# Latent attention of one core: the row probabilities are normalised on GpSimd in place of VectorE

## What is computed

```python
xn = _layernorm(x, axis=-1)
q = (x @ wq).reshape(Bq, Tq, N_KV, N_REP, HEAD_DIM)          # x is xn here; 2 key heads, 4 query heads each
k = einsum('bkhl,ld->bkhd', k_lat, wk_up); v = einsum('bkhl,ld->bkhd', v_lat, wv_up)
scores = einsum('bqhrd,bkhd->bhrqk', q, k) * scale           # Tq = 1024, causal
probs = softmax(where(causal, scores, min), axis=-1)
y = einsum('bhrqk,bkhd->bqhrd', probs, v)
return y.reshape(Bq, Tq, N_HEADS * HEAD_DIM) @ wo
x = x + attention(xn) + six_layers(xn)
```

## Time and profile before

| | |
|---|---|
| median of 3 runs | 1861.76 us |
| span of the profiled execution | 1864.6 us |
| TensorE matmul busy | 1689.0 us (91%) |
| VectorE busy | 1577.2 us (85%) |
| ScalarE busy | 1373.5 us (74%) |
| GpSimd busy | 1395.7 us (75%) |
| latent attention, first to last masked row | 36 to 341 us |

### The profile page before, as it was taken

One profiled execution on the slowest core, in us unless ns is written; L12 is line 12 of the kernel. 1 busy time (PEld: TensorE's weight loads), 2 busy tenths in 40 slices (PEclk: granted clock), 3 DMA queues, 4 the chain that ended last, 5 costly groups with the idle time before them and its releaser, 6 DMA issues.

```text
span 1864.6 us, 74251 instructions
## 1 busy us (share of the span) xinstructions
PE 1689.0 (91%) x31196; PEld 1143.3 (61%) x31196; DVE 1577.2 (85%) x2292; ACT 1373.5 (74%) x2048; POOL 1395.7 (75%) x1493
## 2 busy tenths in 40 slices
PE   6878787788899999999999999999999999999995
PEld 4656666455566666666666566656666666666664
DVE  5867668689898999998999889999899898999973
ACT  3667668466777887788777787788778877887773
POOL 3323223598799888998889888889888889888871
PEclk9999999899999999999999999999999999999997
DMA  4000000001000010000100001000001000000000
GB/s 139 2 0 0 0 1 1 1 28 32 7 7 15 8 56 7 11 15 7 55 7 12 14 7 55 7 7 12 14 30 32 7 12 14 7 8 7 7 7 27
DMA packets 41652, 31.97 MB, mean 17 GB/s; under 512 B 31040, under 2 KB 38912, under 8 KB 39680
## 3 DMA queue, kind: packets, MB, share of 16 engines
q1 hardware_dynamic: 41344, 27.48, 5.0%
HBM read 20.13 MB, written 1.05 MB: 11 GB/s over the span
## 4 chain that ended last, share of the span: by engine, by line
PE 37%; DVE 19%; issue 11%; POOL 7%; ACT 6%; DVEq 0%; POOLq 0%; ACTq 0%
PE banks L1147 15%; PE banks L1401 9%; PE banks L1350 4%; PE banks L1425 4%; PE banks L1386 4%; DVE arena L1012 3%; DVE lnx L1074 3%; DVE small L1041 3%; DVE small L1047 2%; DVE small L1035 2%; DVE small L1059 2%; DVE arena L1007 1%; POOL arena L544 1%; ACT L820 1%; ACT arena L754 1%
## 5 line engine op out<-in xcount | busy, mean ns | idle before, releaser
L1401 PE MATMUL banks<-M,xs 128*32 128x512 f32 x3072 | 369.2, 598 | 0.6 <-ACT arena L754 0.3
L1007 DVE TENSOR_TENSOR arena<-banks,tabs 128x1024 f32<-128x1024 f32 x192 | 233.8, 1218 | 34.1 <-ACT arena L714 17.8
L490 POOL TENSOR_TENSOR arena<-arena 128x1024 f32<-128x1024 f32 x96 | 229.8, 2394 | 43.7 <-DVE arena L1012 43.5
L754 ACT ACTIVATE arena<-banks 128x1024 f32<-128x1024 f32 x192 | 196.9, 1025 | 67.9 <-PE banks L1401 66.8
L1012 DVE TENSOR_TENSOR arena<-banks,tabs 128x1024 f32<-128x1024 f32 x192 | 233.2, 1215 | 0.0
L495 POOL TENSOR_TENSOR arena<-arena 128x1024 f32<-128x1024 f32 x96 | 228.1, 2376 | 0.0
L485 POOL TENSOR_TENSOR prob<-prob,small 128x1024 f32<-128x1024 f32 x96 | 183.8, 1915 | 29.9 <-DVE small L1049 29.9
L1074 DVE SCALAR_TENSOR_TENSOR lnx<-lns,small 128x128 f32<-128x128 f32 x96 | 175.2, 1825 | 34.8 <-POOL small L538 33.7
L1147 PE MATMUL banks<-qkH,xsH 128*128 128x512 f32 x384 | 173.6, 452 | 29.9 <-DVE arena L1012 28.1
L1425 PE MATMUL banks<-arena 128*32 128x128 f32 x6144 | 191.0, 277 | 5.4 <-ACT arena L820 4.2
L410 POOL TENSOR_TENSOR gqs<-arena,cst 128x128 fp32r<-128x128 f32 x112 | 45.1, 403 | 200.9 <-PE banks L1147 171.1
(11 more groups left out here) (123 smaller groups left out, 4033.1 us busy)
## 6 DMA issues: line engine op xcount, KB each, us to landing
arena<-in_wvo_dram SPq DMA_DIRECT2D x6, 1024.0 KB, 5.2
qkraw<-in_wqk_dram SPq DMA_DIRECT2D x6, 1024.0 KB, 5.2
lns<-Xt SPq DMA_DIRECT2D x96, 32.0 KB
lns<-Xt SPq DMA_DIRECT2D x96, 31.8 KB
W<-in_w_dram SPq DMA_DIRECT2D x6, 341.0 KB, 3.4
lns<-Xt SPq DMA_DIRECT2D x84, 0.2 KB
W<-in_w_dram SPq DMA_DIRECT2D x6, 192.0 KB, 3.4
res<-in_x_dram SPq DMA_DIRECT2D x4, 256.0 KB, 3.8
```

What stands on the lines that cost most here:

```text
L490: pool.tensor_tensor(kc, kc, ks, ALU.add).then_inc(s["k_add"], 1)
L754: act.activation(vw[:, (2 * k + g) % RV, :], two(V_BANK), ACT.Copy).then_inc(s[f"v_cp{g}"], 1)
L1007: dve.tensor_tensor(heads(c), heads(two(0)), table(k % NT, kind), ALU.mult).then_inc(s[done], 1)
L1401: ins = pe.matmul(bk(V_BANK + z)[WIN * q:WIN * (q + 1), :], xs[:, b, t0:t0 + WIN], M[:, q, :, :].rearrange("p m n -> p (m n)"), start=True ...
```

## The change

`normalise` leaves VectorE and becomes a GpSimd `tensor_tensor` with the reciprocal broadcast along the row, in the same place in memory. GpSimd's body becomes: the query split of row ahead(j), then the normalisation of row j. The splits of rows 0 and 2 stand ahead of the loop. Nothing else moves; all waits on ls_rec and ls_nrm keep their counts.

```diff
             def latent(it, tables):
-                for k, j in enumerate(apart):
+                def part(j):
+                    k = apart.index(j)
                     i, h = bodies[j]
...
+                def normalise(j):
+                    pr = probs_of(j)[:, 0:(bodies[j][0] + 1) * P]
+                    pool.wait_ge(s["ls_rec"], CR + it * len(bodies) + j + 1)
+                    pool.tensor_tensor(pr, pr, gst[:, 16 + bi(j):17 + bi(j)].to_broadcast([P, pr.shape[-1]]), ALU.mult).then_inc(s["ls_nrm"], 1)
+
+                for j in (0, 2):
+                    part(j)
+                for j in range(len(bodies)):
+                    if ahead(j) in apart:
+                        part(ahead(j))
+                    normalise(j)
...
-                def normalise(j):
-                    pr = probs_of(j)[:, 0:(bodies[j][0] + 1) * P]
-                    dve.wait_ge(s["ls_rec"], CR + it * len(bodies) + j + 1)
-                    dve.tensor_scalar(pr, pr, gst[:, 16 + bi(j):17 + bi(j)], None, ALU.mult).then_inc(s["ls_nrm"], 1)
...
                 for j in range(len(bodies)):
-                    normalise(j)
                     if ahead(j) is not None:
                         cap(ahead(j))
```

More of the change, by code:

```diff
@@ L207, in build @@
             "act": "x_init kk_cp m_cp va_cp wvo_cp gm_cp lq_cp lvl_cp ls_exp lt_cp ly_cp".split(),
-            "dve": "lo_add st_bn st_ag st_eps ln_x0 rs_0 ls_cap ls_max ls_neg ls_rec ls_nrm".split(),
-            "pool": "zeroed gx_H gx_L gq_H gq_L".split(),
+            "dve": "lo_add st_bn st_ag st_eps ln_x0 rs_0 ls_cap ls_max ls_neg ls_rec".split(),
+            "pool": "zeroed gx_H gx_L gq_H gq_L ls_nrm".split(),
         }
```

## The result

The changed kernel takes 1876.45 us (median of 7 runs, 1873.59 to 1879.42), the kernel before 1861.76 us (7 runs, 1856.19 to 1870.29). The ratio is 1.0075, 95% interval 1.0054 to 1.0097: slower, by some 14 us. The profiled execution took 1876.55 us with a span of 1874.7, 10.1 us above the span before.

The account below looks back on a forecast made before the run. A loop of waits, the short normalisation behind the long row's maximum, was taken to bound the kernel. 2.5 us in each of three iterations (7.5) plus 3.7 in the fourth gave +11.2 us, 1873 us; range 1865 to 1881.

Parts of the forecast that it names:

- The price: Normalisation on GpSimd: 0.18 us + 0.00169 us a column, 2.31 us a pair; with two splits 4.05 us a pair.
- The loop of rows (7,0): Long row's finish, scores, mask, reciprocal, GpSimd normalisation: 3.7 us a pair, so +0.3 us for m = 0 to 3.
- m = 4 to 7: Between finishes of long rows 4 and 7: 4.35 us, then two GpSimd-bound pairs of 4.05, sum 12.45 against 12.09, +0.4.
- 11 to 13: Between finishes of long rows 11 and 13: output matmuls on TensorE set the pace before and after, difference 0.
- 13 to 14: Between finishes of long rows 13 and 14: 3.8 us against 4.29, -0.5, the only place where position outweighs GpSimd's slowness.
- The tail: Iteration's end: finish(S_14) 1.9 us later instead of 1.44, +0.45; the last two normalisations hidden behind the next iteration's queries.
- The fourth iteration: Last latent-attention iteration: +3.7 us, including +1.1 at the start and +1.2 for line 424 before L_7's normalisation.
- The signs: Changed profile: GpSimd busy +148 us to about 1543, VectorE about 1508, iteration about 82 us, little GpSimd idle in rows (6,1) to (4,3).
- Absorbed: Rival, chance 0.12: iteration starts and ends take up the lag; only the fourth's 3.7 us or less remain, 1864 to 1865.
- Faster: Rival, chance 0.06: GpSimd's normalisation runs ahead, half of TensorE's 40.9 us of line 940 waits returns: -20 us, 1841.
- Blocked VectorE: Rival, chance 0.05: by the port rule each long normalisation stops a reciprocal or negation: +50 us, 1910.
- GpSimd slower than priced: Rival, chance 0.1: GpSimd needs more than the upper bound, say 4.6 us a pair: +20 us, 1885.

Follow-up runs that it names:

- run 2: The changed kernel with GpSimd multiplying only the first 128 columns of each row, the rest left unnormalised (a probe, not a valid result): 1846.52 us, ratio 0.9905.
- run 6: Against the changed kernel, only the short rows' normalisation on GpSimd, the long rows' on VectorE in its old place, with a second semaphore: 1852.7 us, ratio 0.9951.
- run 8: The kernel before the change with the short row's normalisation moved on VectorE in front of the long row's maximum, GpSimd untouched: 1868.59 us, ratio 1.003.
- run 4: The changed kernel with two GpSimd clears of 128 unused columns behind each long normalisation of the first 13 pairs: 1882.12 us, ratio 1.0095.
- run 1: The changed kernel with the next long row's reciprocal moved on VectorE in front of the short row's mask: 1872.3 us, ratio 1.0045.

## Why the prediction was right, point by point

- **What bounds the kernel.** The short normalisation behind the maximum was a limit, and the place without its price is worth up to 4 us an iteration (run 2). Whether it is fatal depends on who takes it (runs 6 and 8).
- **The price.** 1.91 for 1024 columns measured 1.90, 0.40 for 128 held, as did the line between them; 4.05 us a pair with two splits measured 3.99. Run 4 shows that m = 6 to 7 and 10 to 11 follow GpSimd's load (0.30 and 0.28 for a probe of 0.31), and 5 to 6 and 9 to 10 only in part.
- **The loop of rows (7,0)** was right in its steps and 0.1 too short, 3.7 against 3.82. The mis-sized term is "two hand-overs of about 0.06": they are 0.08 (reciprocal to GpSimd) and 0.13 (GpSimd to TensorE), and the eight transposes keep the next scores 0.93 away, not 0.88. Three pairs make +0.3 of the missing 0.6 us an iteration. Run 1 shows that the loop decided there.
- **m = 4 to 7, 11 to 13, 13 to 14** were each short by 0.1. In 4 to 7 the pair 5 to 6 took 4.17, not 4.05. In 11 to 13 the forecast of nothing rested on TensorE's outputs, and run 4 shows GpSimd there as well. The place where the new position wins most was as forecast, m = 13 to 14, with 0.39 instead of 0.5.
- **The tail** was hidden as said: +0.45 at finish(S_14), and the last two normalisations behind the queries; finish(L_15) came 0.33 us later after finish(L_14) than before.
- **The fourth iteration** was forecast at +3.7 with its start. Without the start 2.6 was forecast and 4.24 measured. Line 424's +1.2 was right (5.36 against 4.14). What the sum lacked is the granted clock of 0.50 at m = 7 to 8: 6.33 against 4.72. Without it the iteration lost 2.6 us, as forecast. TensorE's new wait of 1.63 us stands in front of the lower clock, but run 1 has the same wait without it, so what brings it is open.
- **The total.** 11.2 us forecast, 13.7 in the latent attention of the traces, 14.7 between the medians; 1876.45 lies in the range of 1865 to 1881. Without the two stretches at half clock the traces give 13.1: three iterations of 3.1 in place of 2.5 are the mis-sized part, 1.8 us in all. The forecast had neither these stretches nor the remainder's 3.6 us less, as it put the layers at nothing; that the two profiled spans differ by 10.1, close to the 11.2, is therefore luck. The conversion from span to median (2.8 us) was unsafe: with 1.85 us around the span, as in the changed kernel's profiled execution, that of before would have taken about 1866.4 and was then one of its slower ones.
- **The signs.** GpSimd's busy time grew by 139.7 us instead of 148, VectorE's fell by 55.9 instead of 69. The forecast added up durations of records, and records of neighbouring instructions overlap; the 64 + 64 records of line 940 cover 68.9 us, but 54.4 of these alone. GpSimd had little idle time from m = 5 to 7 and 9 to 12 (at most 0.25 us a pair), but 0.80 us once in rows (5,2), at m = 8, waiting for the short row's reciprocal.
- **Contention.** Reciprocal and negation kept their time beside GpSimd's long instructions: 151 to 165 ns and 153 to 156 ns, as in the earlier trace rows. The port rule of the Trainium skill (SBUF — State Buffer, Who interferes with whom) bears on the multi-column form, which the change took off VectorE; of blocking at one column this trace shows nothing, though 96 of the 128 negations started while an instruction of GpSimd still had 0.2 to 1.68 us to run.
- **Rivals.** *Absorbed* fell: each iteration carried its loss on. *Faster* fell: GpSimd's pair was too long, and the reciprocal came late. Its 40.9 us of waits were also too many to win back: 13.4 of them are weight loads, idle beside TensorE's own 27.5. *Blocked VectorE* and *GpSimd slower than priced* fell with the durations of the lines.

## What to carry to other kernels

An operation that is a wait behind its neighbours in a queue is worth moving by its size: put the small instances on the idle, slower engine, and leave the large ones on the fast engine. Before moving it, add up the other engine's work for one round of the loop, and follow the input too, since a reciprocal that stays behind another row's mask kept the receiving engine idle. And look at what else is in the receiving queue: the 1.28 us of line 424 had cost at most 0.6 us before (m = 6 to 7 of the fourth iteration took 4.14, 3.55 in the others), and cost 1.4 with a long normalisation behind it (5.36 against 3.99). Placed in rows (7,0), where GpSimd idled, it cost nothing in the end.

## What the runs showed of the hardware

- VectorE's multi-column tensor_scalar does slow down beside GpSimd. With short rows on GpSimd the long normalisation on VectorE had a maximum of 1541 ns, against 755 before; this kernel's line 954 and its count, then two of its instructions with GpSimd's beside them:

```profile
L954 DVE TENSOR_SCALAR prob<-prob,small x64: 542/725/1541, 40.4 to 333.6; 128x1024 f32<-128x1024 f32 x16, 128x896 f32<-128x896 f32 x16, 128x768 f32<-128x768 f32 x16, 128x640 f32<-128x640 f32 x16
...
50.17 1.03 DVE L954 TENSOR_SCALAR prob<-prob,small 128x1024 f32<-128x1024 f32 x1
50.18 0.47 POOL L412 TENSOR_TENSOR gqs<-arena,gqs 128x128 fp32r<-128x128 f32 x1
...
301.25 1.54 DVE L954 TENSOR_SCALAR prob<-prob,small 128x896 f32<-128x896 f32 x1
301.02 1.29 POOL L424 TENSOR_TENSOR xsL<-xs,xsH 128x512 fp32r<-128x512 f32 x1
```

  Undisturbed they take 0.75 and 0.68 us in this trace. In each stretched record of this trace the extra time is what GpSimd's instruction still had to run when the VectorE record started, less 0.19 to 0.20 us: 0.28 of 0.48 us in the first pair, 0.86 of 1.06 in the second. By the Trainium skill (SBUF — State Buffer, Who interferes with whom), the later of two instructions on the shared port pair blocks; the stretched records agree, with that offset. Of the 23 that were stretched by more than 40 ns, every one stood beside a query split or line 424 and none beside a short normalisation: the fastest version pays this still, to the work that GpSimd had before. The short normalisation of 1.149 us in the kernel before fits too: line 424 still had 1.00 us to run, and it took 0.81 more than the quickest of its shape.
- The part behind the latent attention, which no kernel changed, took 1522.3 us before, 1518.7 with the change, and between 1511.7 (run 2) and 1520.6 (run 1) in the others, counted from finish(L_15) of the fourth iteration to the end of the span. The medians carry this spread of some ten microseconds, the intervals inside an iteration don't. The time that the granted clock stood at 0.50 in this part goes the same way: in sum 55.3 us before, 41.5 with the change, 50.9 in run 1, 38.0 in run 2. Why it differs from one execution to the next is open.
- The length of an idle time of TensorE does not tell whether its clock falls. In the changed kernel a wait of 1.62 us at 204.67, at the end of the second iteration, was followed by full speed, and one of 1.63 us in the fourth by 1.2 GHz; in the kernel before, 0.93 us at 257.88 was followed by 1.2 GHz, and 1.63 us at 198.48 was not. In run 8 TensorE waited 2.2 us at the end of each of the three iterations, at 99.75, 180.19 and 261.52, and the clock fell behind the second alone. What parts them was not tried.
